# A decoder layer with a routed feed-forward: gate and up in single PSUM banks, and a new order of all engines

## What is computed

```python
x = x + attn(_layernorm(x))                 # 16 heads, rope, causal
x = x + xattn(_layernorm(x), ctx)           # 16 heads, 77 context rows
h = _layernorm(x)
probs = softmax(h @ router_w); top1_val, top1_idx = top of probs
hid = (h @ up_w[e]) * silu(h @ gate_w[e])   # for e = top1_idx, if e < 7
routed = hid @ down_w[e]
shid = (h @ shared_up_w) * silu(h @ shared_gate_w)
x = x + 2.0 * top1_val * routed + shid @ shared_down_w
```

## Time and profile before

| | us |
|---|---|
| median of 3 runs | 1065.71 |
| lowest and highest | 1065.3 and 1066.14 |
| span of the profiled execution | 1065.7 |
| PE busy | 992.5 (93%) |
| DVE busy | 870.9 (82%) |
| ACT busy | 737.2 (69%) |
| POOL busy | 631.4 (59%) |

### The profile page before, as it was taken

How to read it: one execution, slowest core, us unless ns; L and a number is a source line. 1 busy time by engine, 2 the same in 40 slices (tenths; PEclk the granted TensorE clock), 3 DMA queues, 4 the chain that set the end, 5 groups by cost and what they waited for, 6 DMA issues and landing times.

```text
span 1065.7 us, 45022 instructions
## 1 busy us (share of the span) xinstructions
PE 992.5 (93%) x16200; PEld 818.3 (77%) x16201; DVE 870.9 (82%) x2853; ACT 737.2 (69%) x1557; POOL 631.4 (59%) x1488
## 2 busy tenths in 40 slices
PE   1579999999999999999999999999999999999995
PEld 1357777777777777777777777777777889999995
DVE  4367999999999999999999999999986457777774
ACT  0267878888888878888888888887875145555552
POOL 0346677777777677777777777767764124444443
PEclk9999999999999999999999999999999899999998
DMA  6222011000100010000100010000000122222220
GB/s 133 71 72 77 28 32 32 26 30 26 32 26 30 25 29 28 26 30 26 32 26 30 26 29 28 30 25 28 28 29 21 58 70 70 73 71 68 70 65 5
DMA packets 66648, 44.27 MB, mean 42 GB/s; under 512 B 24135, under 2 KB 61451, under 8 KB 66592
## 3 DMA queue, kind: packets, MB, share of 16 engines
q1 hardware_dynamic: 55424, 30.35, 10.5%
q0 software_dynamic: 5312, 12.18, 3.3%
q10 hardware_dynamic: 5856, 0.99, 0.7%
HBM read 23.96 MB, written 18.29 MB: 40 GB/s over the span
## 4 chain that ended last, share of the span: by engine, by line
PE 76%; DVE 10%; issue 4%; SPq 3%; DMA 2%; ACT 1%; POOL 1%; ACTq 1%; DVEq 0%; POOLq 0%
PE pv L1122 11%; PE scores L1302 6%; PE scores L1307 6%; PE ro L1318 6%; PE ro L1177 6%; PE scores L1163 5%; PE st L1232 5%; DVE arena L641 4%; PE scores L999 4%; PE scores L1169 4%; PE ro L1139 3%; PE pj L1145 3%; PE ro L1131 3%; PE ro L1150 2%; PE scores L1033 2%
## 5 line engine op out<-in xcount | busy, mean ns | idle before, releaser
L919 ACT ACTIVATE arena<-scores 128x1024 f32<-128x1024 f32 (+1 forms) x256 | 262.6, 1026 | 48.5 <-PE scores L1016 33.6
L641 DVE TENSOR_REDUCE arena<-scores 128x8 f16<-128x1024 f32 (+1 forms) x256 | 256.7, 1003 | 47.5 <-PE scores L1007 37.6
L859 ACT ACTIVATE arena<-st 128x128 f16<-128x128 f16 (+2 forms) x256 | 154.9, 605 | 7.9 <-PE st L1232 6.8
L859 ACT ACTIVATE arena<-arena 128x512 f16<-128x512 f32 (+2 forms) x192 | 92.9, 484 | 70.3 <-POOL arena L453 50.3
L1122 PE MATMUL pv<-arena 128*32 128x128 f32 (+1 forms) x4096 | 139.3, 277 | 0.0
L1122 PEld LDWEIGHTS pv<-arena 128*32 128x32 f32 (+1 forms) x4096 | 104.6, 110 | 17.1 <-issue 10.1
L439 POOL TENSOR_TENSOR arena<-arena,neg_half 128x1 f32<-128x1 f32 x192 | 106.5, 555 | 15.0
L449 POOL TENSOR_TENSOR arena<-arena 128x256 f32<-128x256 f32 x64 | 46.4, 725 | 78.9 <-DVE arena L633 78.9
L526 POOL DMA_INDIRECT out_dram<-x_tile x70 | 69.9, 998 | 38.5 <-POOL carried L525 26.1
L477 POOL TENSOR_TENSOR arena<-arena 128x128 f32<-128x128 f32 x128 | 51.7, 404 | 61.2 <-DVE arena L651 61.2
L1232 PE MATMUL st<-id,arena 128*128 128x128 f16 (+1 forms) x1024 | 74.0, 215 | 8.5 <-POOL arena L462 8.5
(11 more groups left out here) (175 smaller groups left out, 2681.3 us busy)
## 6 DMA issues: line engine op xcount, KB each, us to landing
x_tile<-xs SPq DMA_DIRECT2D x70, 129.0 KB, 2.0
arena<-arena SPq DMA_DIRECT2D x512, 4.0 KB
arena<-in_x_dram SPq DMA_DIRECT2D x64, 64.0 KB, 1.8
out_dram<-pay SPq DMA_DIRECT2D x64, 64.0 KB, 1.6
arena<-in_ctx_dram SPq DMA_DIRECT2D x64, 38.5 KB
w_gate<-in_L_ffn_gate_w_dram SPq DMA_DIRECT2D x7, 256.0 KB, 2.8
w_up<-in_L_ffn_up_w_dram SPq DMA_DIRECT2D x7, 256.0 KB, 3.1
w_down<-in_L_ffn_down_w_dram SPq DMA_DIRECT2D x7, 256.0 KB, 4.0
```

What stands on the lines that cost most here:

```text
L641: v.tensor_reduce(nmax[:, n, :].rearrange("p (m r s) -> p r m s", r=2, s=SLOT)[:, u, :, 0:HG], pair(s)[:, :, 0:HG * keys].rearrange("p m ( ...
L859: return a.activation(to, of, ACT.Copy)
L919: a.activation(e32[0:rows, 2 * n + u, :], scores[0:rows, 1024 * s:1024 * (s + 1)], ACT.Exp).then_inc(sexp_done[n][u], 1)
```

## The change

The shared gate now writes the bank `ro` and the shared up the bank `st`, each alone; the score pairs hold scores only, pair 0 those for the maxima and pair 1 those for the exponentials. No bank is cut into quarters any more: the short users (transposes, projections, router, positions, values) pass over `pj`, `st`, `pv` and `ro`, each of which has four to six users that follow one another in a step, and one table for each user (`sm1_turns` and the like) names the readers that it waits for.

`positions` loses its matmul with the identity. `run_pos` holds the running counts in SBUF, and `run_of` adds the counts of the batch to them on VectorE, in one operation for both halves; `hot_pos_of` reads SBUF. The marks are found by operations on two tensors, one of them a column that is broadcast (`same_of`, `marks_of`, `hot_of`), in place of operations with a column as pointer scalar. The four `carry` copies go; their waits stand ahead of the instruction before.

The lists of all engines are in a new order, with new lags. A batch enters with lag 0, its qkv projection has lag 1 (2 before), its shared expert lag 9 (8 before), its positions lag 10 (8 before). LATE becomes 60. The stage of the experts is as it was.

```diff
-LAG = 11
-LATE = 56
+LATE = 60
...
-        run_base = sb("run_base", [P, E])
+        run_pos = sb("run_pos", [P, 2, 2 * E])
+        same = sb("same", [P, E])
...
-        st16 = st[:, :].bitcast(F16)
+        pj16, st16, pv16, ro16 = (bank[:, :].bitcast(F16) for bank in (pj, st, pv, ro))
...
-                v.tensor_copy(carried[:, n:n + 1], eps[:, :])
...
+            def same_of(b, p):
+                wait(dve, top_ready, b + 1)
+                v.tensor_tensor(same[:, :], logits[:, p, :], top[:, p:p + 1].to_broadcast([P, E]), ALU.is_equal).then_inc(same_ready, 1)
             def marks_of(b, p):
-                wait(dve, top_ready, b + 1)
-                v.scalar_tensor_tensor(out=mark[:, :], in0=logits[:, p, :], scalar=top[:, p:p + 1], in1=marks,
-                                       op0=ALU.is_equal, op1=ALU.mult).then_inc(marked, 1)
+                v.tensor_tensor(mark[:, :], same[:, :], marks, ALU.mult).then_inc(marked, 1)
-                v.tensor_scalar(hot16[:, p, :], mark[:, :], mark_top[:, :], None, ALU.is_equal).then_inc(hot_ready, 1)
+                v.tensor_tensor(hot16[:, p, :], mark[:, :], mark_top[:, :].to_broadcast([P, E]), ALU.is_equal).then_inc(hot_ready, 1)
...
-            def hot_pos_of(b, p):
-                v.scalar_tensor_tensor(out=hot_pos[:, :], in0=ro[:, 2 * P:2 * P + E], scalar=1.0, in1=hot16[:, p, :],
-                                       op0=ALU.mult, op1=ALU.mult, accum_out=put_f[:, :]).then_inc(hot_posed, 1)
-
             def run_of(b, p):
                 wait(dve, pos_psum, b + 1)
-                v.tensor_copy(run_base[:, :], ro[:, 2 * P + E:2 * P + 2 * E]).then_inc(run_ready, 1)
+                v.tensor_tensor(run_pos[:, p, :].rearrange("p (n e) -> p n e", n=2), run_pos[:, 1 - p, E:2 * E].unsqueeze(1).to_broadcast([P, 2, E]),
+                                pv[:, 0:2 * E].rearrange("p (n e) -> p n e", n=2), ALU.add).then_inc(run_ready, 1)
+
+            def hot_pos_of(b, p):
+                wait(dve, run_ready, b + 1)
+                v.scalar_tensor_tensor(out=hot_pos[:, :], in0=run_pos[:, p, 0:E], scalar=1.0, in1=hot16[:, p, :],
+                                       op0=ALU.mult, op1=ALU.mult, accum_out=put_f[:, :]).then_inc(hot_posed, 1)
 
             def put_of(b, p):
                 wait(dve, hot_posed, b + 1)
                 v.tensor_copy(put[:, place(b, p):place(b, p) + 1], put_f[:, :]).then_inc(put_ready, 1)
 
-            def half_of(b, p, s):
-
+            def half_of(b, p):
                 wait(dve, sh_tanh, b + 1)
-                v.scalar_tensor_tensor(out=half_hid[:, 0, :], in0=tanh_s[:, 0, :], scalar=1.0, in1=scores[:, 1024 * s:1024 * s + F],
+                v.scalar_tensor_tensor(out=half_hid[:, 0, :], in0=tanh_s[:, 0, :], scalar=1.0, in1=ro[:, 0:F],
                                        op0=ALU.add, op1=ALU.mult).then_inc(sh_half, 1)
 
-            def hidden_of(b, p, s):
+            def hidden_of(b, p):
                 wait(dve, sh_half, b + 1)
                 wait(dve, sh_up, b + 1)
-                v.tensor_tensor(hidT[:, 0, :], half_hid[:, 0, :], scores[:, 1024 * s + 512:1024 * s + 512 + F],
-                                ALU.mult).then_inc(sh_hid, 1)
+                v.tensor_tensor(hidT[:, 0, :], half_hid[:, 0, :], st[:, 0:F], ALU.mult).then_inc(sh_hid, 1)
...
+            sm1_turns = (((smax_done[1][1], -3),), ((smax_done[1][0], -3),), ((smax_done[0][0], 0),), ((smax_done[0][1], 0),),)
+            xT1_turns = (((sh_tanh, -4), (sh_half, -4),), ((o_turned[1], -2),), ((qkT_ready, 3),), ((ctxT_ready, 0),), ((xT_ready[1], 0),),)
...
+            def shared_gate(b, p):
...
+                    last = t.matmul(ro[:, c * P:(c + 1) * P], ws_gate[:, c * P:(c + 1) * P], xnT3[:, p, :], start=True, stop=True)
...
+            def shared_up(b, p):
...
-                    last = t.matmul(scores[:, 1024 * s + 512 + c * P:1024 * s + 512 + (c + 1) * P], ws_up[:, c * P:(c + 1) * P], xnT3[:, p, :],
+                    last = t.matmul(st[:, c * P:(c + 1) * P], ws_up[:, c * P:(c + 1) * P], xnT3[:, p, :], start=True, stop=True)
...
+            def positions(b, p):
+                turn(pe, b, *pos_turns)
+                wait(pe, hot_ready, b + 1)
+                cols = pv[:, 0:2 * E].rearrange("p (n e) -> p n e", n=2)
+                t.matmul(cols[:, 0], earlier[:, :], hot16[:, p, :], start=True, stop=False, skip_group_check=True)
+                last = t.matmul(cols[:, 1], ones16[:, :], hot16[:, p, :], start=False, stop=True, skip_group_check=True)
+                last.then_inc(pos_psum, 1)
...
-            def positions(b, p, *users):
-
-                turn(pe, b, *users)
-                wait(pe, hot_ready, b + 1)
-                cols = ro[:, 2 * P:2 * P + 2 * E].rearrange("p (n e) -> p n e", n=2)
-                t.matmul(cols, id32[:, :], run_base[:, :].unsqueeze(1).to_broadcast([P, 2, E]), start=True, stop=False,
-                         skip_group_check=True)
-                t.matmul(cols[:, 0], earlier[:, :], hot16[:, p, :], start=False, stop=False, skip_group_check=True)
-                last = t.matmul(cols[:, 1], ones16[:, :], hot16[:, p, :], start=False, stop=True, skip_group_check=True)
-                last.then_inc(pos_psum, 1)
-
...
-                at(i, p, 8, shared_gate, 0, ((smax_done[0][0], 6),), ((sexp_done[0][0], 5),), ((smax_done[1][1], 3),), ((sexp_done[1][1], 2),), ((sh_hid, 0),))
...
+                at(i, p, 2, stacks)
+                at(i, p, 10, positions)
...
-                at(i, p, 9, token_of)
...
-                at(i, p, 10, scatter)
...
+                at(i, p, 9, scatter)
...
+                at(i, p, 7, token_of)
```

709 lines of the change are left out of this document (401 added, 308 removed).

## The result

| | before | after |
|---|---|---|
| median of 12 runs, us | 1065.26 | 1070.38 |
| lowest and highest | 1061.99 and 1068.59 | 1067.42 and 1074.64 |
| span of the profiled execution | 1065.7 | 1066.8 |

The ratio is 1.0054, with a 95% interval of 1.004 to 1.0069: slightly slower. The prediction was 1024 us with a range to 1050, so the time lies outside it and on the other side of before. The two profiled executions are only 1.1 us apart, the medians 5.1. I account for the profiled pair, which understates the difference.

What follows compares the result with a forecast made beforehand. The prediction took TensorE to bound the loop at 11.95 us a step. Its terms, -0.24 - 0.25 - 0.14 - 0.22 + 0.10 = -0.75, gave 11.20; times 55 steps, -41 us, so 1024 us, range 1002 to 1050.

Steps and rivals of the forecast that it cites:

- The bound of before: Steady loop: TensorE leads, busy 11.74 of 11.95 us a step at full clock, with VectorE close behind at 11.05.
- The identity matmul, -0.24: Positions: dropping the matmul that put running counts into PSUM saves TensorE 0.24 us a step, bounds 0.13 and 0.30.
- Cross projection, self projection, other small waits, -0.61: TensorE's waits at the cross projection (-0.25), self projection (-0.14), and router and score masks (-0.22 together) shrink, us a step.
- All waits go: Rival, chance 0.22: TensorE's waits vanish to their bounds and nothing new appears; -1.04, 10.91 us a step, 1009 us.
- What stays, 0.53: TensorE's 0.53 us a step of waiting for VectorE's add recurs at the turned cross maxima; no gain counted.
- New hand-offs, +0.10: Four single PSUM banks shared by four to six users; tightest in pv at step start, +0.10 us, bounds 0 and 0.53.
- VectorE, 10.3 us, and the marks: Fewer copies and shorter mark operations cut VectorE by 0.75, from 11.05 to 10.3 us a step; slack, no time by itself.
- the rival of the held marks: Rival, chance 0.15: POOL still holds VectorE's new mark operations, 0.36 us on TensorE's path; 11.56 us a step, 1044 us.
- POOL becomes the ring: Rival, chance 0.06: token_of waits for the scatter's landing, delaying layer norms, rope and stacks; 12.3 us a step, 1085 us.
- Fill and drain at zero, -6 to +15: Filling and draining unchanged; a batch's chain is nine steps instead of six, the three more holding little work; -6 to +15 us.
- What would show it: Signs: step 11.0 to 11.4 us, new marks 0.16 to 0.25 us, filling plus draining 155 to 175 us.
- The sign for POOL: Sign in POOL's row: it should stand idle ahead of token_of by less than 0.8 us.

Runs made afterwards that it cites:

- e7: Kernel before with only the identity matmul left out and the running counts added on VectorE; 1066.26 us, ratio 1.0014.
- e12: Changed kernel with token_of behind the third layer norm's reciprocal root, the drain's idle products moved within the step, and add_cross_bias ahead of the scatter; 1041.33 us.
- e14: e12 with the first of the gate's four products made twice, 0.24 us more of TensorE a step; 1054.56 us.
- e8: Kernel before with only the marks changed, to three operations with broadcasts instead of two with a pointer scalar; 1071.2 us, ratio 1.0064.
- e4: Kernel before with all that follows a batch's third layer norm two steps later on every engine; 1078.17 us, ratio 1.0121.
- e9: Kernel before without VectorE's four small carry copies, their waits standing ahead of the entries before them; 1064.94 us, ratio 0.9982.
- e6: Changed kernel with the drain's two idle products moved within the step, behind the up product and behind the transposed third norm; 1063.85 us.
- e5: Changed kernel with POOL's token_of moved behind the third layer norm's reciprocal root, two entries further on; 1065.99 us.
- e2: Kernel before with four slots of pay, put and token, and four steps a loop trip instead of two; 1118.24 us, ratio 1.0507.

## Why the prediction was wrong, point by point

Two steps of the prediction failed above all. In the sum, POOL with the moved scatter stood at nothing (a rival with a chance of 0.06): its two edges hold the step at 11.70 us where the same kernel without them takes 11.27, so they cost 0.43 of the 0.75 us forecast. And filling and draining stood at zero: the drain grew by 26.5 us, more than the loop gained. The terms follow in their order.

**The bound of before.** "TensorE leads" failed too, for the order of before. I read a PE of 98% with gaps as a row whose every matmul counts. e7 shows a matmul of 0.24 us that counts nothing. The prediction asked of each late start who was late, but of the identity matmul it asked only how long it took, not what the next entry needed: the row that ends the argument (hidden until 411.39) was in the trace. A smaller slip: the span of 1065.7 isn't the median of the runs, but about 1.8 us under the time of its own execution, by the other executions.

**The identity matmul, -0.24.** Zero in the order of before. In e12's order TensorE's work counts in full (e14), so it may be worth its 0.24 there; that wasn't tried.

**Cross projection, self projection, other small waits, -0.61.** The named waits went, as forecast. The cross projection starts 0.30 after its predecessor, two passes, without a wait. But the sentence that "the score pairs lose a user, so the masks start with less delay" was wrong. Two score blocks that use the same pairs now have only values and self projection between them, 1.0 + 0.5 us as drawn, while the exponentials take 1.02 and the row maximum 1.22 (durations that none of the prediction's rows held) and begin only when a block's last scores stand. The masks wait 0.34 us a step, 0.18 before. In the rival *All waits go* the small waits stand with -0.32, though the bound was put at -0.43; with it that sum is -1.15.

**What stays, 0.53.** Right: 0.54.

**New hand-offs, +0.10.** Too low, and at the wrong place. I searched the tightest hand-off in bank pv; it lay in the pairs (0.34), in ro (the transposed context, 7.1/42 = 0.17) and at the stacks, 6.0/42 = 0.14. With POOL's edges gone the sum came out nearly right all the same: 11.27 in e12 against 11.20. That it does so with one term worth nothing in before's order and another missing is partly luck.

**VectorE, 10.3 us, and the marks.** Right: 433.39 us busy in the 42 steps from 201.5 to 693.0 us is 10.3. The new operations in the changed kernel, 200 to 700 us (duration min/median/max ns):

```profile
L740 DVE TENSOR_TENSOR same<-logits,top x43: 120/124/130, 203.6 to 695.0; 128x8 f32<-128x8 f32 x43
...
L743 DVE TENSOR_TENSOR mark<-same,consts x43: 122/125/393, 206.4 to 697.8; 128x8 f32<-128x8 f32 x43
...
L751 DVE TENSOR_TENSOR hot<-mark,mark_top x43: 102/103/105, 207.5 to 698.8; 128x8 f16<-128x8 f32 x43
...
L759 DVE TENSOR_TENSOR run_pos<-run_pos,pv x43: 158/170/172, 208.2 to 699.6; 128x16 f32<-128x16 f32 x43
```

Not held, but for some of L743 (0.39). So the rival of the held marks fell. It is the place in the row that frees them, not the form: e8 has the same form held at 0.53. In the changed kernel `same` runs just ahead of the rope add:

```profile
413.71 0.12 DVE L740 TENSOR_TENSOR same<-logits,top 128x8 f32<-128x8 f32 x1
```

```profile
413.83 0.73 POOL L463 TENSOR_TENSOR arena<-arena 128x256 f32<-128x256 f32 x1
```

That is near what the prediction itself had against this rival: POOL is late, and `same` meets a short operation, the reciprocal root L447 (128x1, 413.32 to 413.87). Where L743 takes 0.39, at 416.48, it ends with a 128x128 operation of POOL (L474, 416.42 to 416.85). The Trainium skill (SBUF — State Buffer, Who interferes with whom) has a VectorE instruction of two SBUF inputs contend with a GpSimd instruction that reads SBUF. The trace agrees for e8's first mark (0.53 beside a rope add, against 0.12 for the same operation in the changed kernel), but not for L740 beside L447, which reads SBUF too and holds nothing up.

**POOL becomes the ring.** The mechanism of this rival was right: token wait, then layer norms, rope and stacks behind it. Two things were wrong. The condition "binds from a token wait of 0.8 us" was worked out from POOL's idle sum, 11.20 - 8.57 - 1.84. That sum takes POOL's other waits as fixed and free, but the largest of them, for `put`, is itself part of the ring: a late scatter makes a late `put`. The ring held the step with a wait of 0.52. And I looked for one edge out of the moved scatter; there were two. Three entries now stand between the scatter and the token, and I priced only the entry that names the scatter's semaphore, not the one whose count VectorE waits for (`add_cross_bias`, which stood ahead of the scatter before). The price was wrong too, by the other sign: 11.70, not 12.3 us a step.

**Fill and drain at zero, -6 to +15.** The drain took 26.5 us more. Two steps of depth are worth 14.0 (e4 against e8 and e9), the place of the idle products 7.4 (e6), the lower clock that came with it included; before's own drain had lost 2.7 to the clock. 14.0 + 7.4 - 2.7 makes 18.7; 7.8 us stay open. Where they lie can be read: e6 and e4 both take 17.6 us from the last gate to the first expert product, but the fourth to seventh of the eight steps ahead take 11.9, 9.9, 9.7 and 8.4 us from gate to gate in e6, and 8.6, 8.8, 7.3 and 7.1 in e4. The third step that I counted, from the gate to the positions in the next step, costs 0.9 us: that last stretch is 17.8 us before and 18.7 in the changed kernel. The token moved in e5 shortens the drain by 4.1 us too, but adds nothing to e6's move (99.2 in e12, 99.4 in e6), so I don't count it. "The three more hold little work" was true and beside the point: in the drain a step costs what its chain of waits takes, 7 to 10 us, not what it holds.

**What would show it.** The prediction named as its root error that "PE waits in several banks of the new order by 0.2 us or more each, or if the drain grows by 20 us". The second came in full, the first in part. The sign for POOL, an idle time of under 0.8 us ahead of the token, was met with 0.52 while POOL held the step; it was no test of this rival.

## What to carry to other kernels

Before a matmul is counted as gained, read what the next entry on the engine needs and when that was ready; a full row with no visible wait may be one in which the work just covers the wait. When an instruction with a late release is moved up an in-order row, list every entry that it now stands ahead of, and for each of them every engine that waits on its count; and as several such edges can hold the step in turn, taking one away may show nothing. A step of depth in a software pipeline is paid once in the drain, at the length of the step's chain of waits, so it belongs in the sum beside what it saves in each step.

## What the runs showed of the hardware

**A longer loop body.** Four steps a trip instead of two cost 53 us in the kernel before (e2), with the same work in the same order. Its DMA queues (packets, MB, share of 16 engines) and two of its waits, 200 to 700 us:

```profile
q8 instruction: 142, 2.33, 0.9%
```

```profile
PEld pj L1140 <- issue: 25.2, 9, 3.1
```

The instruction queue moved 142 packets, in the kernel before with its two-step loop 36; nine times in 500 us the transpose of the input waited about 2.8 us for nothing that the profile names. Most steps between the stalls take 11.9 to 12.1 us. The Trainium skill (Runtime: NRT & Kernel Launch, Instruction fetch mechanics) says that a taken branch to a target outside the engine's small instruction window has to fetch it before going on. The trace agrees in kind: the body of two steps runs without such stalls, that of four doesn't. That each stall is such a fetch is argued from the packets; no run shows it.

**The clock.** In e4's drain TensorE was busy 7.80 and 7.83 us in stretches of 10 us (837 to 857) at a granted clock of 1.00; in the drain of the changed kernel it was busy 7.82 us in one such stretch (821 to 831) at 0.66. So the busy share of a stretch alone doesn't tell the clock there. Nor does it compare the work: matmuls last longer at the lower level, and the 7.82 us are 40 records of matmuls where e4's are 70 and 67.
